# A decoder layer on one core: attention outputs moved by transfers, and the middle of each group in a new order

## What is computed

```python
# self-attention (q, k rotated; k, v repeated for the 4 query heads of each key head)
q = (x @ Wqa @ Wqb).reshape(b, s, H, D)
kv = (x @ Wkva @ Wkvb).reshape(b, s, KVH, D, 2)
scores = jnp.where(causal, -jnp.inf, einsum('bqhd,bkhd->bhqk', q, k) * scale)
out = einsum('bhqk,bkhd->bqhd', softmax(scores), v).reshape(b, s, E)
return out @ Wout + bout
# cross-attention: the same with q from x, k and v from ctx, and the mask in place of the causal one
# feed-forward
h = relu(x @ w1.T + b1)
out = float_quantize(quantised(h) @ quantised(w2).T + bq)
# the layer
x = x + self_attention(layernorm(x))
x = x + cross_attention(layernorm(x), ctx, ctx, mask)
x = x + feed_forward(layernorm(x))
```

## Time and profile before

| | us |
|---|---|
| median of 3 runs | 1822.03 (1814.67 to 1822.35) |
| profiled execution, its own time | 1819.02 |
| its span in the profile | 1817.0 |
| TensorE busy | 1673.7 (92%) |
| VectorE busy | 1245.2 (69%) |
| ScalarE busy | 1103.6 (61%) |
| GpSimd busy | 724.2 (40%) |
| transfer engines, busy share of the page's second part | 0.2 to 0.7 of 16 in most slices |

### The profile page before, as it was taken

How to read it: one execution, slowest core, us unless ns; L and a number is a source line. 1 busy time by engine, 2 the same in 40 slices (tenths; PEclk the granted TensorE clock), 3 DMA queues, 4 the chain that set the end, 5 groups by cost and what they waited for, 6 DMA issues and landing times.

```text
span 1817.0 us, 34264 instructions
## 1 busy us (share of the span) xinstructions
PE 1673.7 (92%) x12274; PEld 1015.8 (56%) x12274; DVE 1245.2 (69%) x1908; ACT 1103.6 (61%) x1704; POOL 724.2 (40%) x962
## 2 busy tenths in 40 slices
PE   3779999999999999999999999999999999999987
PEld 1445556556555565555556555665655556555554
DVE  4567486785848768586776848678585876858582
ACT  3355675756667565665756567575666756566572
POOL 3251353624435352433634345362443535243310
PEclk9979999999999999999999999999999999999998
DMA  6452552715346251633724255271534625163320
GB/s 170 59 83 39 76 88 36 122 28 85 57 64 100 36 95 38 92 67 43 121 36 79 49 75 88 36 119 30 84 59 62 101 36 95 37 93 57 48 37 12
DMA packets 86606, 124.07 MB, mean 68 GB/s; under 512 B 10481, under 2 KB 53938, under 8 KB 86322
## 3 DMA queue, kind: packets, MB, share of 16 engines
q1 hardware_dynamic: 83650, 115.26, 41.5%
q0 software_dynamic: 2160, 7.87, 1.2%
q10 hardware_dynamic: 768, 0.57, 0.1%
HBM read 21.42 MB, written 8.39 MB: 16 GB/s over the span
## 4 chain that ended last, share of the span: by engine, by line
PE 68%; DVE 10%; issue 7%; ACT 5%; POOL 4%; DMA 3%; SPq 2%; ACTq 0%; POOLq 0%
PE o_pair L1318 12%; PE small L1404 8%; PE small L1149 7%; DVE negmax L900 6%; PE score L1279 6%; PE o_pair L1149 3%; PE small L1331 3%; PE small L1165 3%; PE score L1256 3%; DMA Q<-negT 2%; PE small L1435 2%; PE score L1202 2%; DVE P L922 2%; PE score L1261 2%; ACT P L691 2%
## 5 line engine op out<-in xcount | busy, mean ns | idle before, releaser
L691 ACT ACTIVATE P<-score 128x1024 f32<-128x1024 f32 x448 | 446.8, 1026 | 119.7 <-PE score L1279 42.7
L900 DVE TENSOR_REDUCE negmax<-score 128x4 f32<-128x1024 f32 (+1 forms) x384 | 460.0, 1219 | 32.6 <-PE score L1237 19.8
L922 DVE TENSOR_TENSOR P<-P,cross_bound 128x1024 f32<-128x1024 f32 x192 | 255.6, 1365 | 65.8 <-ACT P L691 65.6
L1318 PE MATMUL o_pair<-P,V 128*32 128x256 f32 (+1 forms) x4096 | 283.1, 363 | 15.6 <-DVE P L922 15.6
L737 ACT ACTIVATE score<-cross_q 128x1024 f32<-128x1024 bf16 x192 | 196.5, 1023 | 60.3 <-DVE negmax L900 58.7
L468 POOL TENSOR_TENSOR negrest<-negmax,negparts 128x32 f32<-128x32 f32 x64 | 15.5, 243 | 502.1 <-ACT negparts L652 501.6
L1318 PEld LDWEIGHTS o_pair<-P,V 128*32 128x32 f32 x4096 | 86.2, 108 | 148.2 <-issue 78.1
L1279 PE MATMUL score<-Q,K 99*128 99x256 bf16 x1024 | 151.5, 275 | 13.3 <-DMA Q<-negT 12.2
L1435 PE MATMUL small<-xnT,w 128*128 128x256 f32 x600 | 156.7, 379 | 0.0
L1237 PE MATMUL score<-K,Q 96*128 96x256 bf16 x768 | 119.5, 279 | 33.8 <-ACT score L737 30.8
L1279 PEld LDWEIGHTS score<-Q,K 99*128 99x128 bf16 x1024 | 85.8, 98 | 100.8 <-issue 66.1
(11 more groups left out here) (181 smaller groups left out, 3219.4 us busy)
## 6 DMA issues: line engine op xcount, KB each, us to landing
Q<-q1p SPq DMA_DIRECT2D x96, 256.0 KB, 5.9
K<-k2p SPq DMA_DIRECT2D x96, 256.0 KB, 8.4
Q<-q2p SPq DMA_DIRECT2D x192, 128.0 KB, 4.0
x_in<-in_x SPq DMA_DIRECT2D x16, 512.0 KB, 5.6
ctxT<-in_ctx SPq DMA_DIRECT2D x16, 512.0 KB, 4.4
k2f<-q1f SPq DMA_DIRECT2D x32, 256.0 KB, 5.3
out_y<-x POOLq DMA_DIRECT2D x15, 512.0 KB, 3.6
K<-k1p SPq DMA_DIRECT2D x96, 64.0 KB, 4.5
```

The lines of the kernel that those rows point to most:

```text
L691: A.activation(P[:, t % 4, :], score[b][:, :, :], ACT.Exp, scale=SCALE).then_inc(score_free[b], 1)
L900: V.tensor_reduce(negmax[:, k, h:h + 1024 // w], s.rearrange("p (h w) -> p h w", w=w), AX.X, ALU.max, negate=True).then_inc(score_free[b], 1)
L922: V.tensor_tensor(p, p, cross_bound[:, t % 2, :].unsqueeze(1).broadcast_to([128, 4, SEQ]), ALU.min).then_inc(probs_masked[1], 1)
L1318: last = T.matmul(o_ps[ob][32 * j:32 * j + 32, SEQ * gg + q0:SEQ * gg + SEQ], v, p, start=s == 0, stop=end, tile_position=(0, 32 * j), ski ...
```

## The change

- **Outputs.** The turns of the units and of `o` are gone, but for the last group's cross-attention, which keeps them. V has its values in the even columns and ones in the odd ones, so that the even rows of a copied-out unit are the heads' outputs and every odd row repeats the sum of its head. SyncE copies the 64 even rows to `inT` or `oT` and one sum for each head to `sums` (two transfers a unit). VectorE inverts `sums`, 32 rows of 256 queries for the cross-attention and 16 rows for each batch of the self-attention. SyncE spreads each inverse over the 16 rows of its head (`over_sum`, an alias of `o`), two transfers a batch. The product is made by VectorE for the self-attention (`over_sums1`) and by GpSimd for the cross-attention (`over_sums`). The rows of `Wout` and `wo` are laid out to fit.
- **Work moved.** The context's values are copied by ScalarE without a bias (the bias goes through `wo` into `bo2` once at the start). The second key tile's subtraction goes from VectorE to GpSimd, from a full copy that ScalarE makes.
- **Middle.** TensorE asks for both `o_pair` banks right behind the pass, does the norms' turns and tile 0 ahead of `out1_0`, and has tiles 1 and 2 in halves between the small products, and tile 3 there too. `PIECES` holds four tiles in place of five.
- **Start.** The mask and w2 are loaded first, the first group's queries are rotated, cut and stacked by sequence (batch 0 first), and the first keys are stacked through GpSimd's queue.
- **End.** The last group's output, norm, feed-forward tiles and output are done by sequence.

```diff
-    attention = (["k2_0"] + p("m2T_1", "o2t0", "o2t1", "o2t2", "o2t3")
-                 + ["v2_0", "k2_1", "m1T_0"] + p("oT2_0", "oT2_1") + p("out2_0", "out2_1")
-                 + ["v2_1", "m1T_1", "o1t0", "o1t1", "oT1_0", "o1t2"])
-    middle = (["out1_0"] + p("xnT3_0", "xnT3_1") + ["o1t3"] + n("xnT1_0", "xnT1_1") + p("h0") + ["oT1_1"]
-              + n("qa") + ["xnT2_0", "out1_1", "q2_0"] + n("q0", "q1") + n("k", "v_0", "v_1")
-              + p("h1") + ["xnT2_1"] + p("h2") + ["q2_1"])
-    scores = p("h3", "h4", "h5", "h6", "h7") + ["m2T_0"] + p("ffn0", "ffn1")
+    attention = (["k2_0"] + p("m2T_1") + ["v2_0", "k2_1", "m1T_0"] + p("out2_0", "out2_1")
+                 + ["v2_1", "m1T_1"])
+    middle = (p("xnT3_0", "xnT3_1") + n("xnT1_0", "xnT1_1") + p("h0") + ["out1_0"] + n("qa") + p("h1") + n("q0")
+              + n("q1") + ["xnT2_0", "out1_1", "q2_0"] + n("k") + p("h2") + n("v_0", "v_1") + ["xnT2_1"] + p("h3")
+              + ["q2_1"])
+    scores = p("h4", "h5", "h6", "h7") + ["m2T_0"] + p("ffn0", "ffn1")
     return over(2, attention) + over(4, middle, 1) + over(2, scores)
...
-        PIECES = (2, 2, 1, 2, 2, 2, 2, 2, 1, 2, 2, 0)
-        assert sum(PIECES) == 4 * (HT - 3)
-        EVICT_AFTER = (4, 6, 8, 11, 12)
+        PIECES = (2, 1, 1, 2, 1, 1, 2, 1, 1, 2, 2, 0)
+        assert sum(PIECES) == 4 * (HT - 4)
+        EVICT_AFTER = (4, 7, 10, 12)
...
+            def put_outputs2(g, u):
+
+                bank, before = o_bank(1, g, u)
+                b, gp = u // 2, u % 2
+                sp.wait_ge(o_free[bank], before + 1)
+                sp.dma_start(inT[64 * gp:64 * gp + 64, :, SEQ * b:SEQ * b + SEQ],
+                             o_sb[0:128:2, u % 2, :].rearrange("p (c q) -> p c q", c=NC)).then_inc(o2_moved[u % 2], 16)
+                sp.dma_start(sums2[8 * u:8 * u + 8, :], o_sb[1:128:32, u % 2, :]).then_inc(o2_moved[u % 2], 16)
+
...
+            def put_outputs1(g, u):
+
+                bank, before = o_bank(0, g, u)
+                b, gp = u // 2, u % 2
+                row = 32 * b + 8 * gp
+                sp.wait_ge(o_free[bank], before + 1)
+                sp.dma_start(sums[row:row + 8, :], o_sb[1:128:32, u % 2, :]).then_inc(o1_moved[u % 2], 16)
+                sp.dma_start(oT[64 * gp:64 * gp + 64, :, SEQ * b:SEQ * b + SEQ],
+                             o_sb[0:128:2, u % 2, :].rearrange("p (c q) -> p c q", c=NC)).then_inc(o1_moved[u % 2], 16)
+
+            def put_inverses1(g, b):
+
+                sp.wait_ge(inverse1_ready[b], g + 1)
+                for c in range(NC):
+                    sp.dma_start(over_sum[:, c, SEQ * b:SEQ * b + SEQ],
+                                 inverse[32 * b + c:32 * b + 16:2, :].unsqueeze(1).broadcast_to([8, HD, SEQ])
+                                 ).then_inc(inverse1_moved[b], 16)
+
...
+            def put_inverses2(g):
+
+                sp.wait_ge(inverse2_ready, g + 1)
+                for b in range(GB):
+                    for c in range(NC):
+                        sp.dma_start(over_sum[:, c, SEQ * b:SEQ * b + SEQ],
+                                     inverse2[16 * b + c:16 * b + 16:2, :].unsqueeze(1).broadcast_to([8, HD, SEQ])
+                                     ).then_inc(inverse2_moved[b], 16)
+
...
+                    for u in range(UNITS):
+                        put_outputs2(i - 1, u)
+                    put_inverses2(i - 1)
+                put_neg(st, 0, 0)
+                for n in range(2):
                     put_part("k2", n, i)
+                put_neg(st, 0, 1)
+                put_part("k2", 2, i)
+                for u in range(2):
+                    put_outputs1(i, u)
+                put_inverses1(i, 0)
+                for u in range(2, UNITS):
+                    put_outputs1(i, u)
+                put_inverses1(i, 1)
                 for b in range(GB):
                     for n in range(3):
                         put_query2(n, b, i)
@@ -411,9 +485,9 @@
...
+            def over_sums(g, b):
+
+                for n in range(2):
+                    pool.wait_ge(o2_moved[n], 32 * (UNITS // 2) * (g + 1))
+                pool.wait_ge(inverse2_moved[b], 16 * NC * (g + 1))
+                at = slice(SEQ * b, SEQ * b + SEQ)
+                G.tensor_tensor(inT[:, :, at], inT[:, :, at], over_sum[:, :, at], ALU.mult).then_inc(o2_whole, 1)
+
+            def keys_rest(st, g):
+
+                pool.wait_ge(small_free[st.bank("k2_1")], st.this("k2_1"))
+                G.tensor_tensor(k2f[:, 1, :], k2f[:, 1, :], k2p[:, 0, 1, :], ALU.subtract).then_inc(rest1["k2"], 1)
...
+                keys_rest(st, i)
+                if prev:
+                    for b in range(GB):
+                        over_sums(i - 1, b)
                     add_bias2(i - 1)
                 cut_rest(0, i, 1)
...
+            def keys_full(st, c):
 
                 bk = st.bank(f"k2_{c}")
-                act.wait_ge(small_free[bk], st.this(f"k2_{c}"))
+                A.activation(k2f[:, c, :], small[bk][:, :], ACT.Identity,
+                             bias=bk2[:, c:c + 1]).then_inc(small_free[bk], 1)
+
+            def values2(st, r):
+
+                bk = st.bank(f"v2_{r}")
+                act.wait_ge(small_full[bk], st.this(f"v2_{r}"))
+                A.activation(V2[:, 2 * r:2 * r + 2, :, 0:32:2],
+                             small[bk][:, :].rearrange("p (k h n) -> p k h n", k=2, n=HD),
+                             ACT.Copy).then_inc(small_free[bk], 1)
...
-                    if u >= 2:
+                    if u >= 2 and not last:
+                        act.wait_ge((o1_moved, o2_moved)[a][u % 2], 32 * (g * (UNITS // 2) + u // 2))
+                    elif u >= 2:
                         name = f"o{a + 1}t{u - 2}"
                         act.wait_ge(small_full[st.bank(name)], st.before(name) + 1)
...
+            def inverted1(g, b):
+
+                for n in range(2):
+                    dve.wait_ge(o1_moved[n], 32 * (g * (UNITS // 2) + b + 1))
+                rows = slice(32 * b, 32 * b + 16)
+                V.reciprocal(inverse[rows, :], sums[rows, :]).then_inc(inverse1_ready[b], 1)
+
+            def over_sums1(g, b):
+
+                dve.wait_ge(inverse1_moved[b], 16 * NC * (g + 1))
+                at = slice(SEQ * b, SEQ * b + SEQ)
+                V.tensor_tensor(oT[:, :, at], oT[:, :, at], over_sum[:, :, at], ALU.mult).then_inc(o1_whole, 1)
 
...
-                    if prev and t in (1, 4):
-                        normalise(st, 1, 2 if t == 1 else 3, i - 1)
+                    if prev and t == 3:
+                        for n in range(2):
+                            dve.wait_ge(o2_moved[n], 32 * (UNITS // 2) * i)
+                        V.reciprocal(inverse2[:, :], sums2[:, :]).then_inc(inverse2_ready, 1)
                     if not prev and t == 2:
                         keys_rest(st, i, 0)
-                    if t == 5:
-                        values2(st, 0)
...
                 attend(st, 0, i, None)
-                unit_turn(st, 0, i, 2)
-                batch_copied(st, "oT1_0")
-                tokens(st, "out1", oT, wout, 0)
                 banks_given(i)
                 if prev:
                     pe.wait_ge(xn_ready[2], i)
                     for c in range(NC):
                         turned(st, f"xnT3_{c}", xn, c)
-                unit_turn(st, 0, i, 3)
                 if nxt:
                     pe.wait_ge(xn_ready[0], i + 2)
                     for c in range(NC):
@@ -1535,28 +1698,37 @@
                 if prev:
                     copied(st, "xnT3_")
                     hidden(st, [0])
-                heads_turned_batch(st, 1)
+                pe.wait_ge(o1_whole, GB * i + 1)
+                tokens(st, "out1", oT, wout, 0)
                 if nxt:
                     latent(st)
+                if prev:
+                    hidden_half(st, 1, 0)
+                if nxt:
+                    pe.wait_ge(small_free[st.bank("qa")], st.this("qa"))
+                    query1(st, 0)
+                if prev:
+                    hidden_half(st, 1, 1)
+                if nxt:
+                    query1(st, 1)
                 pe.wait_ge(xn_ready[1], GB * i + 1)
                 turned_batch(st, "xnT2_0", 0, xn)
-                batch_copied(st, "oT1_1")
+                pe.wait_ge(o1_whole, GB * i + 2)
                 tokens(st, "out1", oT, wout, 1)
                 batch_copied(st, "xnT2_0")
                 query2(st, 0)
                 if nxt:
-                    pe.wait_ge(small_free[st.bank("qa")], st.this("qa"))
-                    for c in range(NC):
-                        query1(st, c)
                     key1(st)
+                if prev:
+                    hidden_half(st, 2, 0)
+                    hidden_half(st, 2, 1)
+                if nxt:
                     for r in range(2):
                         value1(st, r)
-                if prev:
-                    hidden(st, [1])
                 pe.wait_ge(xn_ready[1], GB * i + 2)
```

(2 more changed lines are left out.)

416 lines of the change are left out of this document (248 added, 168 removed).

## The result

| | before | after |
|---|---|---|
| median of the runs, us | 1822.2 (4 runs, 1814.7 to 1823.5) | 1964.5 (4 runs, 1963.7 to 1967.1) |
| profiled span, us | 1817.0 | 1962.0 |
| ratio, with its 95% interval | | 1.079 (1.076 to 1.082) |

The changed kernel is slower by 142 us. The forecast was 1777, so it missed by 187 us, and on the other side.

What follows compares the result with a forecast made beforehand. TensorE's work, 92% busy, was taken as the bound. Period 106.8 - 1.0 + 0.3 + 1.1 - 1.2 = 106.0 against 107.9; span 1817 - 27 (loop) - 10.5 (start) - 7.5 (end) = 1772, time 1777 us, range 1720 to 1832.

Steps and rivals of the forecast that it cites:

- the clock's fall: TensorE's drop to 1.2 GHz for some 3.5 us behind the latent's small key and value products; taken as gone.
- Removed work: TensorE in each group: 12 sets of four transposes at 0.49 us go, 5.9 us less.
- Prices of the links: New chain: output pair 3.0 us, spread pair 3.9, reciprocal 1.9, product 0.69 on VectorE or 1.2 to 1.3 on GpSimd.
- rival 3: Transfers land late, 4.0 us output and 5.9 spread pairs: 1847 us, chance 0.20; sign: output product waits 3 us and more.
- Cross-attention, second pass: 569.9 to 593.8: two turns go where TensorE sets the pace, -1.0 us a group.
- Self scores: 593.8 to 612.0: four turn sets go, but VectorE's wait and GpSimd's queue take it back, +0.3 us.
- Self pass: 612.0 to 629.8: three turn sets and a wait go, -1.9 us.
- Middle: 629.8 to 653.4: output products wait for the new chain; +1.1 us against the undisturbed stage, the pass's 1.9 included.
- First and last group: Longer new chain (some 24 us against 20 to 22) offset by shorter other stages: 0.
- End: Last group's tiles by batches, first half about 5 us earlier, second norm hidden: -7.5 us, bounds -3 and -12.
- Rival 1: Chains stay hidden, reciprocal 0.25 us and landings 2.2, so the sum's waits vanish: 1713 us, chance 0.15.
- Rival 2: Clock falls again once in every group because TensorE pauses at two to four places: 1802 us, chance 0.15.

## Why the prediction was wrong, point by point

**What bounds the kernel.** Right for the kernel before, and the step that failed stands there: "So what counts is TensorE's work, and any new wait that a change puts in its way". I looked for such waits only where the new chain ends. The maxima rows share SyncE's order with the new transfers, and their place against the key copies was changed; the sum has no term for them. Any copy that TensorE wants within a few us should have been listed with the bytes that are issued ahead of it, and shortly behind. The earlier trace rows had the figure for that: 0.73 of the transfer engines' time in the stretch of the self pass, where the keys drain, in the kernel before. A second term was put at nothing: "I take the clock's fall as gone". It came in more places, behind the new waits: the mean granted clock was 0.943, and 0.981 before.

**Removed work.** 5.9 us a group fits: with all copies small TensorE is busy for 82.7 us less than before (1591.0 for 1673.7), 5.2 in each of 16 groups. The period is 103.4 us, 4.5 below the mean of before, with 0.85 of wait for the last copy-out and other new waits in it.

**Prices of the links.** The reciprocal took 1.742 us (1.9 forecast, and a little above that in rival 3; it is below both), the products 0.692 and 1.264 (0.69; 1.2 to 1.3). The output pair took 3.5 us, not 3.0, and the pair of spread copies 4.6, not 3.9; both are the same with all old copies small (622.10 to 625.63, and 4.65 above), so this is a price that was wrong and not a backlog. VectorE's timeline:

```profile
671.69 1.74 DVE L1069 RECIPROCAL inverse<-sums 16x256 f32<-16x256 f32 x1 [9.65 <-DMA q2f<-o_sb]
678.08 0.69 DVE L1075 TENSOR_TENSOR q2f<-q2f,o 128x512 f32<-128x512 f32 x1 [4.65 <-DMA o<-inverse]
```

The pair issued at 668.15 frees the reciprocal at 671.69, and the spread pair issued at 673.46 the product at 678.08. At an eighth of the bytes both take 2.6 us (601.55 and 604.88 are issues, 607.45 the reciprocal; 609.22 to 611.83 the spread pair, in the trace with all copies small), so 2 us of a spread pair go with seven eighths of its data. The estimate that stood beside my price, by the Trainium skill (SBUF — State Buffer, "Door 1: The DMA port swizzle"), was 4.6 for the pair; the measurement agrees with it, and not with mine.

**Cross-attention, second pass.** Forecast -1.0, measured -0.2: the turns went, and waits for maxima rows of 2.2 and 0.5 us came, with a time at the lower clock behind the first.

**Self scores.** Forecast 18.5, measured 18.2. The mechanism held: VectorE waited for the bias row (2.49 us), TensorE's value product 0.18 and not 0.5.

**Self pass.** Forecast -1.9, measured +4.0. This is the greatest miss, 5.9 us a group: TensorE idles for 3.5 us (21.80 less 18.34), 3.1 of them for the rows, and is busy for 2.4 longer than forecast, with a granted clock of 0.84 in this stretch and 1.00 before.

**Middle.** Forecast 24.8, measured 28.8. The first output product waited 1.6 us for 1.2 forecast, the second 0.5, the scores 1.4 for the first batch's queries, where I had called it a draw. With the old copies small and the new ones whole, the whole period is 107.4, 1.4 above the forecast of 106.0: my prices of the new links, 0.5 and 0.7 too low in this stage, account for about that much. The other 10.2 of the 11.6 us a period are the old copies' bytes, for which the sum had no term.

**First and last group.** Forecast 0. The first scores start at 43.28 instead of 51.97 (-8.7, forecast -10.5), but the second cross pass of group 1 starts at 140.13 against 139.56: the first group takes all of it back. From the last start of the loop to the end's it is 115.5 us (1786.55 to 1902.06) against 101.8. TensorE's timeline in the last group:

```profile
1855.99 1.99 PE L1563 MATMUL small<-wout,q2f 128*128 128x256 f32 x8 [1.58 <-DVE q2f L1075]
...
1863.11 1.12 PE L1511 MATMUL o_pair<-ident,xn 128*128 128x128 f32 x4 [3.42 <-DVE xn L1033]
...
1874.38 0.66 PE L1511 MATMUL o_pair<-ident,xn 128*128 128x128 f32 x4 [2.16 <-DVE xn L1033]
```

Without the next group's latent, queries and keys little covers the chain. TensorE's waits in this group sum to 18.2 us, 6.1 before; 3.2 of them are for the maxima rows of the self pass, so not all of it is the chain. "The new chain is longer than the old one ... and their other stages shorter: 0" was a draw declared without a count; it is +9 and +14 us.

**End.** -5.0 (55.9 from the last start of the cross pass to the last product, 61.0 before), forecast -7.5, within its bounds.

**The sum.** Loop 11.6 x 14 = 162, first group and start 11, last group 14, end 2.5: 190 us, and the span missed its forecast of 1772 by 190. The time missed by 187, as it lies 2.5 us over the span and not 5.

**Rivals.** Rival 3 (each transfer lands late) was nearest, with 0.20 and 1847: the cause was of its kind, but I priced it by the queue as it is without the change (4.0 and 5.9 us) and only on the new transfers. Its sign did not come in the group shown: the first output product waited 1.6 us, not 3 and more. Rival 1 fell with the reciprocal at 1.742 us. Rival 2's clock falls came too, behind the new waits. Nothing in the range allowed for old transfers to become late.

## What to carry to other kernels

Before a transfer is added to a busy program, list the small ones that an engine waits for, and with each the bytes issued ahead of it in every queue and still under way, and, as no run here clears them, those issued within 1 or 2 us behind it. Here it landed 2.5 to 3.8 us after the bytes ahead had drained at some 115 GB/s. A bulk copy that costs nothing where it stands (1.000 with and without its bytes) costs 146 us in a new order with small copies around it, and 142 when the new copies among these carry next to nothing (1906.7 less 1764.4). An order for them is found by splitting the bulk (-77 us), not by moving it whole (+25, +74). And a wait that is removed lets the next one show: count the bytes to the end of the stage.

## What the runs showed of the hardware

- A copy of 24 KB alone in ScalarE's queue took 9.3 us while SyncE's queue had 256 KB copies under way: a queue of its own gave a small copy no precedence. In those 9.3 us 1.2 MB moved, of which 0.8 had been issued ahead of it.
- Copies of 256 KB within SBUF drained at about 115 GB/s with the transfer engines full, in slices of 103 to 129 GB/s. That is the rate of these copies and not the engines' own: the slice at 648 in the same view holds 201 GB/s.
- Spreading 8 rows to 128 partitions, two copies of 128 KB: 4.6 us, whether the old copies are whole or small; 2.0 of it go with seven eighths of the bytes.
- TensorE's clock was at 1.2 GHz for some us behind the wait of 3.09 us at 661.45 (products of 1.08 us for 0.64) and behind that of 2.20 at 608.82 (four products of 3.23 us for 1.88); the mean granted clock was 0.943 in the changed kernel, 0.975 with all copies small.

What stays open: whether the changed loop can be ordered below 107.9 us a period with all its bytes. The best that was tried is 111.7 (split keys, later input); its waits for cross maxima rows (29.9 us) and outputs (36.8 us) remain. Why the same five copies ahead of the rows cost 0.8 us in the old kernel and 3.1 in the new one is open too, beyond the moments at which they are issued and wanted, and so is how the 5.3 us a period of the old copies other than the keys divide among the waits.
